# The last chunk's output projection: its own PSUM banks, and its matmuls in two parts

## The reference

```python
x = x + attn(layernorm(x))            # q, k, v, rope, softmax(q k / 4) v, then out @ Wo.T + bo
x = x + ffn(layernorm(x))             # below
# ffn:  xc = bf16(x); normed = xc * rsqrt(mean(xc^2) + eps) * norm_weight
#       logits = normed @ gate.T + gate_bias; top 2, softmax -> combine
#       g, lin = min(p1[even], 7), clip(p1[odd], -7, 7)      with p1 = normed @ mlp1.T + bias
#       act = g * sigmoid(1.702 g) * (lin + 1);  p2 = act @ mlp2.T + bias
#       out = xc + bf16(sum over experts of combine * p2)
```

## Time and profile before

| | |
|---|---|
| Timed runs, median | 1109.83 us |
| Profiled execution, its own time | 1114.86 us |
| Its span, first to last instruction | 1113.0 us |
| TensorE busy | 951.1 us, 85% |
| VectorE busy | 767.6 us, 69% |
| ScalarE busy | 747.4 us, 67% |
| GpSimd busy | 422.8 us, 38% |

### The profile page before, as it was taken

How to read it: one execution, slowest core, us unless ns; L and a number is a source line. 1 busy time by engine, 2 the same in 40 slices (tenths; PEclk the granted TensorE clock), 3 DMA queues, 4 the chain that set the end, 5 groups by cost and what they waited for, 6 DMA issues and landing times.

```text
span 1113.0 us, 16680 instructions
## 1 busy us (share of the span) xinstructions
PE 951.1 (85%) x5288; PEld 399.5 (36%) x5288; DVE 767.6 (69%) x1528; ACT 747.4 (67%) x1017; POOL 422.8 (38%) x357
## 2 busy tenths in 40 slices
PE   4729899899888997989889998889989999996564
PEld 1402223234342443334343443334443443344243
DVE  5641111588758885698758786588867886787897
ACT  2428886877668785877668686777868887782232
POOL 3413302443364424543264434543331333334252
PEclk9859999999999998999899999999999999998587
DMA  5362446244435452444435243444534453421110
GB/s 163 91 156 53 107 85 134 72 106 106 109 90 137 103 110 75 111 107 115 110 91 136 77 106 88 109 100 108 126 78 115 105 125 82 106 82 48 48 50 27
DMA packets 79987, 109.81 MB, mean 99 GB/s; under 512 B 22530, under 2 KB 56722, under 8 KB 76818
## 3 DMA queue, kind: packets, MB, share of 16 engines
q1 hardware_dynamic: 61460, 83.47, 32.3%
q10 hardware_dynamic: 18432, 25.17, 7.7%
HBM read 82.90 MB, written 25.69 MB: 98 GB/s over the span
## 4 chain that ended last, share of the span: by engine, by line
PE 58%; DVE 16%; ACT 9%; issue 9%; POOL 3%; DMA 3%; SPq 1%; ACTq 0%; DVEq 0%; POOLq 0%
PE OP L722 16%; PE S L708 15%; PE D L694 8%; ACT probs L844 4%; PE A L677 4%; PE D L596 4%; PE BB L677 4%; PE D L618 3%; DVE th_sb L1150 2%; PE D L610 2%; DVE acc L1145 2%; DVE l_sb L1135 2%; DVE g_sb L1133 2%; DMA o_scr<-O 1%; ACT sqs L807 1%
## 5 line engine op out<-in xcount | busy, mean ns | idle before, releaser
L844 ACT ACTIVATE probs<-S 128x1024 f32<-128x1024 f32 x512 | 513.4, 1025 | 171.5 <-PE S L708 170.4
L708 PE MATMUL S<-Qs,Ks 98*128 98x512 bf16 x1024 | 303.5, 389 | 31.1 <-ACT probs L844 16.2
L722 PE MATMUL OP<-probs,V 128*17 128x512 f32 x2048 | 275.5, 610 | 3.6 <-ACT O L853 3.6
L931 POOL TENSOR_TENSOR act_lo<-act_sb,act_hi 128x512 fp32r<-128x512 f32 x128 | 170.7, 1336 | 153.4 <-ACT act_hi L833 151.0
L708 PEld LDWEIGHTS S<-Qs,Ks 98*128 98x128 bf16 x1024 | 79.4, 99 | 216.9 <-ACT probs L844 100.0
L694 PE MATMUL D<-W,act_hi 128*128 128x256 f32 x448 | 133.0, 329 | 25.6 <-issue 14.7
L1145 DVE SCALAR_TENSOR_TENSOR acc<-D,combh,acc 128x256 f32<-128x256 f32 x224 | 97.6, 477 | 81.2 <-PE D L694 80.7
L1150 DVE SCALAR_TENSOR_TENSOR th_sb<-th_sb,g_sb 128x512 f32<-128x512 f32 x128 | 121.5, 950 | 17.0 <-ACT th_sb L820 13.3
L925 POOL TENSOR_SCALAR W<-W2b 128x512 fp32r<-128x512 bf16 x64 | 43.5, 680 | 197.3 <-PE D L694 192.0
L694 PE MATMUL D<-W,act_lo 128*128 128x256 f32 x448 | 114.3, 286 | 0.0
L833 ACT CAST act_hi<-act_sb 128x512 fp32r<-128x512 f32 x128 | 78.3, 612 | 51.8 <-DVE act_sb L1155 46.2
(11 more groups left out here) (156 smaller groups left out, 989.5 us busy)
## 6 DMA issues: line engine op xcount, KB each, us to landing
W<-in_w ACTq DMA_DIRECT2D x64, 256.0 KB, 2.7
Ks<-k_scr SPq DMA_DIRECT2D x32, 384.0 KB
W2b<-in_w ACTq DMA_DIRECT2D x64, 128.0 KB, 2.8
Ks<-k_scr SPq DMA_DIRECT2D x32, 256.0 KB
o_scr<-O SPq DMA_DIRECT2D x32, 256.0 KB, 4.2
Qs<-q_scr SPq DMA_DIRECT2D x32, 192.0 KB
k_scr<-parts SPq DMA_DIRECT2D x12, 384.0 KB, 3.4
q_scr<-parts SPq DMA_DIRECT2D x12, 384.0 KB, 3.0
```

Source lines behind the costliest of these rows:

```text
L708: last = mm(S[:, j2, C * i:C * (i + 1)], Ks[0:SROWS + MROWS, g % 2, j, P * kt:P * (kt + 1)], Qs[0:SROWS + MROWS, g % 2, j, :], start=True, ...
L722: last = mm(OP[32 * j:32 * j + VW, :], V[:, kt, HG * g + j, :], probs[:, s % 2, C * j:C * (j + 1)], start=kt == 0, stop=kt == KT - 1)
L844: nc.scalar.activation(probs[:, s % 2, 2 * C * j2:2 * C * (j2 + 1)], S[:, j2, :], ACT.Exp, scale=SCALE).then_inc(exp_done, 1)
L931: tt(act_lo[:, e % 2, it, :], act_sb[:, a % 2, :], act_hi[:, e % 2, it, :].bitcast(FP32), ALU.subtract).then_inc(lo_s, 1)
```

## The change

The first channel half of chunk 7's output projection becomes a stage of its own, `wo_0`, at half 8, between up 15 and down 12 in TensorE's queue; it covers both halves of the tokens. The stages `wo0` and `wo1` keep the second channel half. For chunk 7 the four token tiles get a bank of S each (the first 256 columns of it), and TensorE no longer waits for bank D ahead of wo0 and wo1. Ahead of `wo_0` it waits that all exponentials are done (they read S) and for channel half 0 of Op. VectorE adds from two banks of S in one instruction. The other chunks issue the same matmuls as before.

```diff
     AT = {...
-          "guard": 4, "flag": 6, "x1_in": 0, "x1_b": 11, ...
+          "guard": 4, "flag": 6, "x1_in": 0, "wo_0": 8, "x1_b": 11, ...
...
-    for st in ("x1_in", "x1_b", "stats2", ...
+    for st in ("x1_in", "wo_0", "x1_b", "stats2", ...
...
+        def wo_bank(u, a, bank):
+
+            if alone(u):
+                return S[:, a, :].rearrange("p (t c) -> p t c", t=2)[:, :, 0:E]
+            return bank[:, :].rearrange("p (t c) -> p t c", t=2)
...
-                if st in FILLS and filling[1] and (st != "guard" or n == NCH - 1):
+                if st in FILLS and filling[1] and (st != "guard" or n == NCH - 1) and not (st == "wo" and alone(u)):
                     pe.wait_ge(*read_of(*filling[1]))
...
+                elif st == "wo_0" and alone(u):
+                    pe.wait_ge(exp_done, PAIRS * B * NCH)
+                    pe.wait_ge(on_s, 2 * u + 1)
+                    project_out(0, u, (0,), None)
+                    project_out(1, u, (0,), None)
                 elif st == "wo":
                     pe.wait_ge(on_s, 2 * (u + 1))
-                    for t in range(2):
-                        tok = P * (2 * a + t)
-                        for c in range(CT):
-                            last = mm(bank[:, E * t:E * (t + 1)], Op[:, c, tok:tok + P], wo_sb[:, c, :],
-                                      start=c == 0, stop=c == CT - 1)
-                    last.then_inc(d_full, 1)
+                    project_out(a, u, (1,) if alone(u) else range(CT), bank).then_inc(d_full, 1)
...
+            def project_out(a, u, parts_in, bank):
+
+                for t in range(2):
+                    tok = P * (2 * a + t)
+                    for c in parts_in:
+                        last = mm(wo_bank(u, a, bank)[:, t, :], Op[:, c, tok:tok + P], wo_sb[:, c, :],
+                                  start=c == 0, stop=c == CT - 1)
+                return last
...
-                    xh = X1s[:, n, 2 * a:2 * a + 2, :].rearrange("p t c -> p (t c)")
-                    v.tensor_tensor(xh, bank[:, :], xh, ALU.add).then_inc(x1_s, 1)
+                    xh = X1s[:, n, 2 * a:2 * a + 2, :]
+                    v.tensor_tensor(xh, wo_bank(u, a, bank), xh, ALU.add).then_inc(x1_s, 1)
```

More of the change, by code:

```diff
@@ L74, in block_kernel @@
         place(PREP, h + AT["length"] + AT[st], (st, 0))
-    for st in ("x1_in", "x1_b", "stats2", "rstd2", "xc", "ss", "ms", "rrms", "nf", "nfT", "logits", "gates1", "etop",
+    for st in ("x1_in", "wo_0", "x1_b", "stats2", "rstd2", "xc", "ss", "ms", "rrms", "nf", "nfT", "logits", "gates1", "etop",
                "gates2", "combT"):
```

## The result

| | before | changed |
|---|---|---|
| Median of 20 timed runs each, us | 1110.20 (1108.16 to 1115.04) | 1106.26 (1102.02 to 1110.10) |
| Profiled execution, own time and span | 1114.86, 1113.0 | 1105.45, 1103.7 |

The ratio is 0.996, 95% interval 0.9948 to 0.9972: the change gains 3.1 to 5.8 us. The forecast was 2.6 us less (1107.2, range 1104.9 to 1109.2), most probably within 0.3%.

What follows compares the result with a forecast made beforehand. The bound was taken to be seven TensorE-VectorE links through bank D ahead of stats2. 2.96 us, less 0.25 (GpSimd held) and 0.1 (late downs), made 2.6: 1109.83 to 1107.2 us, range 1104.9 to 1109.2.

Steps and rivals of the forecast that it cites:

- within 0.3%: Whole kernel: median between 1106.5 and 1113.2 us, not to be told from no change; chance 0.66.
- The chain through D, and what replaces it: Path to stats2: TensorE-VectorE waits through bank D go, GpSimd's bias releases the first add; stats2 2.7 us earlier.
- the sum: Whole kernel: 2.96 us at stats2, less 0.25 and 0.1, makes 2.6 us gained; median 1107.2.
- wo_0's price: Early stage at half 8: its 8 records take 2.01 us at the high clock.
- The 0.25 us passed to GpSimd: Around the scaling of Op: act_sb 0.25 us later makes GpSimd's scaling, act_lo and bias end 0.25 later.
- Down 14 and down 15: Behind stats2: at the low clock both could move ms by up to 0.4 us; 0.1 taken as lost.
- The last term, the tail: Stretch from stats2 to the end: no change beyond the 0.1 us taken for the downs.
- rival A: Tail: the last 16 down records run at the high clock, 1.65 us more gained, 1105.6; chance 0.22.
- C: Experts of chunk 7: VectorE and GpSimd meet at 0.69 all seven times, 3.0 us more, 1110.2; chance 0.05.
- the prediction's own signs of being wrong: Two-bank adds well over 0.7, act_sb's delay not passed to GpSimd, or stats2 to end differing by over 1 us.
- A's own price: End of the tail: the last 16 down records take 2.15 us at the high clock instead of 3.80, 1.65 less.
- Rival B: Early stage: wo_0 finds the low clock and takes 3.66 us; only 0.85 us gained, 1109.0; chance 0.13.

Runs made afterwards that it cites:

- second look: The changed kernel again, unaltered, for a second trace; ratio of times to the kernel before 0.9962 (0.9944 to 0.9980).
- third look: The changed kernel once more, unaltered, for a third trace; ratio of times to the kernel before 0.9970 (0.9951 to 0.9989).
- bias_at_8: Changed kernel with GpSimd adding the last chunk's bias at half 8, ahead of the scaling of Op, instead of half 11; ratio to before 0.9950.
- late_2: Changed kernel with two unused GpSimd multiplications (2.54 us) put ahead of the last chunk's bias; ratio to before 0.9966 (0.9948 to 0.9984).
- banks_only: Changed kernel without its early stage: wo0 and wo1 keep 8 records each in the four score banks; ratio to before 0.9955 (0.9938 to 0.9971).
- bias_matmul: Changed kernel with the early stage at half 11 and the last chunk's bias added by TensorE matmuls, not GpSimd; ratio to before 0.9963.
- before_third: The kernel before once more, unaltered, for a fourth trace of its form; ratio to before 0.9999 (0.9982 to 1.0016).

## Why the prediction was right, and where it was off

- *The chain through D, and what replaces it.* Right, and tested both ways: the first add is released by GpSimd in all three traces of the changed kernel, stats2 moved by 2.7 us (24.64 to 21.90) in the pair of profiles, the term of the sum. Over four and three traces nf moved from 33.39 to 30.77: 2.62, against the 2.6 of the sum. That the figures agree so closely is in part luck. In the pair the scaling of Op began 0.5 us earlier after the copy of O than before, the scaling and act_lo together took 0.8 longer, and the adds cost 0.1 less. In the other two traces stats2 came at 21.6, which is 3.0 less than the 24.64 that the sum was made on, so the sum without its 0.25; and 24.64 is the longest of the four of before (24.09 to 24.64).
- *wo_0's price.* 1.89 us at clock 1.00 against 2.01 in the sum. Down 12's first record starts 1.5 us behind wo_0's start, where the sum had 1.88, so the time that VectorE spends on other evictions hides all of it.
- *The 0.25 us passed to GpSimd failed as a step.* wo_0 delays VectorE by nothing: down 12 is evicted at 13.33 in the second and the third look. The scaling takes 1.27 there. In the pair VectorE was 0.6 late for another reason, th_sb's meeting ahead of wo_0, and the scaling took 0.37 and act_lo 0.46 more than before. That the two engines hold each other is right: the scaling takes 1.46, 1.37, 1.28 and 1.27 in the four traces of before, the less, the later it starts against act_sb. The Trainium skill (GPSIMD Engine Reference, section 1, Specifications) says that GpSimd's SBUF interfaces are shared with VectorE, with contention for Vector instructions of two SBUF inputs. The trace of bias_at_8 agrees: 2.86 us for a th_sb of 0.68, behind a bias of 2.37.
- *Down 14 and down 15.* Down 15 came 0.45 us late for VectorE in the changed kernel, 0.38 before, and from stats2 to nf it was 9.02 us in both: of the 0.1 taken, nothing was lost. In the second look, where both downs had the low clock (2.09 each), it was 9.17, so 0.15 was lost.
- *The last term, the tail, is what failed.* The sum had it unchanged and left the clock to rival A, at 0.22, and worse meetings of VectorE and GpSimd to C, at 0.05. In the runs the mean tail went from 78.57 (four) to 77.60 (three), 1.0 us, with 76.95 to 78.57 in the three. One of the prediction's own signs of being wrong was met: from stats2 to the end it was 87.56 before and 86.30 in the changed kernel, 1.3 us less (87.7 and 86.0 in the other two). It is A's cause (the clock changes at other moments relative to the work) and C's mechanism with the sign turned: the th_sb of 1.37 is gone in two of the three, and the last downs take 3.36 to 3.79 instead of 3.80. A's own price, a last pair wholly at the high clock, was seen in none of the three. I took the tail of one profile for a mean that could move either way; it was the long end of what occurs, and before has it every time.
- *The size.* 2.6 and 1.0 make 3.6 us by the traces; the times say 3.1 to 5.8, 2.2 to 6.2 and 1.2 to 5.4. So "within 0.3%" with 0.66 was wrong by the 1.0 us of the tail, at a forecast that lay only 0.7 us from the bound.
- *Open.* Rival B was seen in no trace (an early stage of 8 records took 1.89 us in each of the eight that have one). The times of late_2 (1.8 to 5.8 us gained) and banks_only (3.2 to 6.9) are larger gains than O to the end gives in their traces, 1.4 and 1.5 (110.56 and 110.42 against a mean of 111.96 for the four of before). These two profiles were the slowest runs of their kernels (1113.42 and 1109.41 against medians of 1108.62 and 1106.64), and the part ahead of the last copy of O took 995.1 to 1000.8 in the form before and 993.9 to 1001.0 in the others. Whether some 1 to 2 us come from there, with the same instructions but for the form of the access patterns, can't be told from one trace each. So the traces show what the change does to stats2 and nf; that the time gained is made of that and the tail alone isn't shown. No kernel isolates it.

## What to carry to other kernels

When a wait between two engines is taken off the chain, look at every other condition of the instruction that waited: here the bias on GpSimd, hidden by 0.9 us before, became the bound at once, and it is that row, not the matmul time saved, that gave the right size of 2.7 us. Work whose inputs are early is worth splitting off: with the banks free already, the early half of the matmuls gave 2.0 us more in a trace at the low clock, where the free banks alone gave 0.6; at the high clock it may give far less. A forecast near a decision bound should use several traces of the kernel before, as the tail of one of them may be an extreme.

## What the runs showed of the hardware that I had not expected

- fp32 matmuls that contract over one row (the bias) in turn with such over 128 rows went slower than the latter alone: 16 alternating records took 5.1 us, 0.32 each, at clock 1.00, where 8 records over 128 rows took 1.89, 0.24 each. Why isn't shown. The stretch with its clock in bias_matmul:

```profile
1012.00:1014.00 2.00, 2.00 (x9) 1.06 (x7) 0.68 (x1) 0.62 (x1) 1.38 (x2) 1.00 0.49 180
```

- One VectorE instruction that reads two PSUM banks with 256 columns each costs the same as one that reads 512 of one bank: 0.68 and 0.69 in the changed kernel, 0.69 in bias_matmul, and 0.69 from one bank before.
- The moments of the clock's changes were the same to 0.5 us in four executions of the form before up to 38 us after nf (one of them, before_third, differs later), and the rise between 15 and 25 us came up to 3 us earlier in the other forms.
